# Second relational convolution of a graph network: running softmax maximum, attention dots from PSUM, first probabilities among the last product tiles

## The reference, cut to what matters

```python
def rgat_conv(x, W, q, k, b, src, dst, etype, heads, out_ch, n_nodes):
    xr = jnp.einsum('nd,rdf->rnf', x, W)
    oi = xr[etype, dst]
    oj = xr[etype, src]
    qi = oi @ q
    kj = oj @ k
    alpha = jax.nn.leaky_relu(qi + kj, NEG_SLOPE)
    m = jax.ops.segment_max(alpha, dst, num_segments=n_nodes)
    e = jnp.exp(alpha - m[dst])
    z = jax.ops.segment_sum(e, dst, num_segments=n_nodes)
    a = e / (z[dst] + EPS)
    msg = (a[:, :, None] * oj.reshape(-1, heads, out_ch)).reshape(-1, heads * out_ch)
    out = jax.ops.segment_sum(msg, dst, num_segments=n_nodes)
    return out + b
```

## Time and profile before

| | us |
|---|---|
| median of 3 runs | 1986.36 (1985.3 to 1987.12) |
| the profiled execution's own time | 1985.76 |
| its span | 1983.9 |
| PE busy | 1797.8 (91%) |
| DVE busy | 1300.2 (66%) |
| ACT busy | 725.5 (37%) |
| POOL busy | 711.7 (36%) |

### The profile page before, as it was taken

The page is one execution under the profiler, slowest core; times in us unless marked ns, Lnnn a source line. Parts: engine busy times, 40 slices in busy tenths (PEclk is TensorE's granted clock), DMA queues, the critical chain, the costliest instruction groups (busy, mean ns, idle before and its releaser), DMA issues. The chain is left out here.

```text
span 1983.9 us, 26904 instructions
## 1 busy us (share of the span) xinstructions
PE 1797.8 (91%) x8995; PEld 1504.9 (76%) x8997; DVE 1300.2 (66%) x2159; ACT 725.5 (37%) x1170; POOL 711.7 (36%) x386
## 2 busy tenths in 40 slices
PE   8999888999999998979886778688999999999887
PEld 3444685999999997868864578587788888899866
DVE  9998476887887886577399868665442422444545
ACT  0213544445444443323566534313224223332231
POOL 1665231422423331314766557311324233332411
PEclk9999999999999999979997889699999999999989
DMA  1002522222312221224200022012222222222230
GB/s 19 22 0 110 217 96 80 93 69 64 111 64 67 92 79 32 58 79 143 81 16 1 0 75 93 25 51 78 83 69 72 90 86 83 90 83 91 80 112 33
DMA packets 54199, 143.08 MB, mean 72 GB/s; under 512 B 13780, under 2 KB 13908, under 8 KB 53076
## 3 DMA queue, kind: packets, MB, share of 16 engines
q1 hardware_dynamic: 46898, 107.15, 17.5%
q10 hardware_dynamic: 7202, 34.63, 4.8%
HBM read 129.18 MB, written 12.58 MB: 71 GB/s over the span
## 5 line engine op out<-in xcount | busy, mean ns | idle before, releaser
L734 POOL TENSOR_TENSOR w_pair<-early,w_pair 128x768 fp32r<-128x768 f32 x234 | 450.2, 1953 | 921.0 <-ACT w_pair L1253 920.8
L789 PE MATMUL ps<-w_pair,cols_x 128*128 128x384 f32 x2160 | 390.8, 339 | 13.7 <-POOL cols_x L734 13.7
L789 PEld LDWEIGHTS ps<-w_pair,cols_x 128*128 128x128 f32 x2160 | 379.0, 190 | 18.5 <-POOL cols_x L734 14.1
L789 PE MATMUL ps<-w_pair,wide 128*128 128x384 f32 x1872 | 335.3, 339 | 13.1 <-DVE wide L1622 11.7
L789 PEld LDWEIGHTS ps<-w_pair,wide 128*128 128x128 f32 x1872 | 330.9, 191 | 17.5 <-DVE wide L1622 13.0
L1253 ACT ACTIVATE w_pair<-early 128x768 fp32r<-128x768 f32 x234 | 181.2, 840 | 341.8 <-PE ps L789 156.3
L1199 PE MATMUL ps<-wide,w_pair 128*128 128x512 f32 x972 | 224.9, 390 | 2.2 <-DVE wide L1622 2.2
L1199 PEld LDWEIGHTS ps<-wide,w_pair 128*128 128x128 f32 x972 | 181.5, 188 | 39.8 <-DVE wide L1622 2.6
L428 PE MATMUL count_ps<-early,src_hot 128*128 (+1 forms) x814 | 179.3, 382 | 7.9 <-DVE early L348 7.7
L428 PEld LDWEIGHTS count_ps<-early,src_hot 128*128 (+1 forms) x816 | 80.2, 98 | 106.5 <-issue 9.6
L1167 PE MATMUL ps<-prob,wide 128*128 128x512 f32 x588 | 149.4, 394 | 0.0
(11 more groups left out here) (239 smaller groups left out, 2450.6 us busy)
## 6 DMA issues: line engine op xcount, KB each, us to landing
early<-weights SPq DMA_DIRECT2D x240, 384.0 KB, 3.1
multi<-attn ACTq DMA_DIRECT2D x9, 768.0 KB, 4.5
...
kept<-early ACTq DMA_DIRECT2D x3, 1536.0 KB, 6.0
multi<-kept ACTq DMA_DIRECT2D x3, 1536.0 KB, 6.5
...
src_hot<-weights SPq DMA_DIRECT2D x10, 384.0 KB, 7.0
...
```

The lines of the kernel that those rows point to most:

```text
L734: return nc.gpsimd.tensor_tensor(dst, whole, high.bitcast(F32), ALU.subtract)
L789: mm = nc.tensor.matmul(ps[:, m, 0:HW], left[:, a, k, m * P:(m + 1) * P], w_pair[:, slot_of[0], b, k, :], start=(k == 0 and a + b == 0), s ...
```

## The change

Five things change in this layer:

1. **Dots from PSUM** (`product_dots` for `split_tile`): DVE reads bank m itself, after ACT's copies; the scratch output moves to `acc`. ACT no longer waits for the dots before it copies the next tile, and PE waits for the dots (`rows_ready`) before it writes a bank anew.
2. **Running maximum**: logits of relations 0 and 1 are finished among the tiles of relation 2, with the maximum of these two alone. The maximum with relation 2 (`greatest(2)`) comes during the row sums of relation 0. The difference of the two is exponentiated on ACT (`fade`), and scales the sums and denominators of relations 0 and 1 when those of relation 2 are added.
3. **Early u, v and probabilities**: u and v of relations 0 and 1 are transposed and spread among tiles 4 to 7 of relation 2; three exponents and two weighings of relation 0 stand among the dots of its tiles 6 and 7.
4. **Relation 2's source, maxima, u and v** move between the quarters of the row sums (`small` in `row_sums`), and DVE reads the banks in halves around its other work.
5. **Weights**: POOL's low parts of blocks 44 and 45, and ACT's high part of block 45, move behind the probabilities of relation 1. SP's load of a piece of block 45 follows POOL's piece of block 44, as before.

```diff
@@ uv_sets2
-        uv_sets2 = [(r_den[:], v_bc[:]), tuple(mask[:, 2 * i:2 * i + 2, :].rearrange("p m n -> p (m n)").bitcast(F32) for i in range(2))]
+        uv_sets2 = [(r_den[:], v_bc[:]), (acc_flat[:, 2 * D:2 * D + N], acc_flat[:, 2 * D + N:2 * D + 2 * N])]
@@ gpsimd
-                        if m == 3:
+                        if m == 3 and first_pass + 2 * r + n < 44:
                             weights_low(n, 3 * (first_pass + 2 * r + n))
...
+                if t == 2 * NB - 1:
+                    weights_low(0, 3 * 44)
+                    weights_low(1, 3 * 45)
@@ tensor
+                    if r or n:
+                        pe.wait_ge(rows_ready, 64 + 8 * r + 4 * n - 4 + m + 1)
...
-            for part in range(2):
-                max_round(12, 33, part)
-
-            pe.wait_ge(uv_ready, 11)
-            for r in range(REL3):
-                if r:
-                    pe.wait_ge(vb_ready, 21 + r)
-                turn_small(uvc[:, r, 0], 4)
-                pe.wait_ge(q_ready, 34 + r)
+                    if r == 2 and u == 4:
+                        pe.wait_ge(uv_ready, 11)
+                        turn_small(uvc[:, 0, 0], 4)
+                    elif r == 2 and u == 5:
+                        pe.wait_ge(q_ready, 33)
+                        spread_uv()
+                    elif r == 2 and u == 6:
+                        pe.wait_ge(vb_ready, 22)
+                        turn_small(uvc[:, 1, 0], 4)
+                    elif r == 2 and u == 7:
+                        pe.wait_ge(q_ready, 34)
+                        spread_uv()
...
+            row_sums(rows[0], prob_sets[0], 140, tile_copied, 109, 8, {2: last_source, 3: spread_last_source})
+            pe.wait_ge(den_read, 2)
+            pe.wait_ge(rows_low, 40)
+            row_sums(rows[1], prob_sets[1], 144, row_read, 13, 16, {1: turn_last_uv, 2: spread_last_uv})
@@ scalar
-                    copy_tile(38 + 2 * r + n, m, n, 88 + 8 * r + u, rows[r], lows=24 + 8 * r + u, dots_done=64 + 8 * r + u - 1)
-                    if m == 3:
+                    copy_tile(38 + 2 * r + n, m, n, 88 + 8 * r + u, rows[r], first=True, lows=24 + 8 * r + u)
+                    if m == 3 and 2 * r + n < 5:
                         split_high(40 + 2 * r + n, n)
...
+                    if r == 2 and u == 4:
+                        copy_rows(74, 4)
+                    elif r == 2 and u == 5:
+                        copy_uv(75, uv_sets2[0])
+                    elif r == 2 and u == 6:
+                        copy_rows(76, 4)
+                        exponentials(0, 0, 1)
+
+            exponentials(0, 1, NB + 1)
+            act.wait_ge(rows_ready, 88)
+            copy_uv(77, uv_sets2[1])
+            act.wait_ge(prod_done, 4 * 44)
+            exponentials(1)
+            copy_rows(78, 2)
+            split_high(45, 1)
+            act.wait_ge(fade_in, 1)
+            nc.scalar.activation(mx1[:, 1, 0], mx1[:, 1, 0], ACT.Exp).then_inc(fade, 1)
+            copy_rows(81, 4)
+            copy_uv(82, uv_sets2[0])
+            act.wait_ge(row_done, 16)
+            exponentials(2)
@@ vector
-                add(acc[:, m, part], acc[:, m, part], ps[:, m, 0:HW]).then_inc(row_read, 1)
+                nc.vector.scalar_tensor_tensor(acc[:, m, part], acc[:, m, part], mx1[:, 1, 0, m:m + 1], ps[:, m, 0:HW],
+                                               ALU.mult, ALU.add).then_inc(row_read, 1)
...
+            def product_dots(r, u):
+
+                n, m = u // 4, u % 4
+                part = slice(n * HW, (n + 1) * HW)
+                dve.wait_ge(tile_copied, 88 + 8 * r + u + 1)
+                dve.wait_ge(rows_ready, 64 + 8 * r + u)
+                for v in range(2):
+                    total = al1[:, v, r, 0, m:m + 1]
+                    start = 0.0 if n == 0 else al_part[:, v, m:m + 1]
+                    ins = dot(dot_scratch[v], ps[:, m, 0:HW], acc[:, v, part], start, al_part[:, v, m:m + 1] if n == 0 else total)
+                    ins.then_inc(rows_ready, 1) if v else mark(ins)
+                wait_steps()
...
+                    if r == 2 and u == 6:
+                        probabilities(0, 0, 2)
+                    elif r == 2 and u == 7:
+                        probabilities(0, 2, 3)
+                    product_dots(r, u)
                     if r and u == 2:
                         dve.wait_ge(rows_ready, 64 + 8 * r + u + 1)
-                        maxima(70 + 2 * (r - 1) + 1, mx1[:, r - 1, 0], 21 + r, 140)
+                        relation_logits(r - 1, 70 + 2 * (r - 1) + 1, 21 + r, 140)
+                        if r == 2:
+                            greatest(1)
+                            mark(relation_parts(0, mx[:]))
+                            relation_parts(1, mx[:]).then_inc(uv_ready, 1)
...
+            source_columns(al1[:, 0, 2, 0])
+            probabilities(0, 3)
+            probabilities(1)
+            read_denominators(79, True)
+            read_rows(0, range(NB))
             dve.wait_ge(mask_in, 16 * 6)
+            relation_logits(2, 80, 24, 148)
+            read_rows(0, range(NB, 8))
+            greatest(2)
+            sub(mx1[:, 1, 0], mx1[:, 1, 0], mx[:]).then_inc(fade_in, 1)
+            relation_parts(2, mx[:]).then_inc(uv_ready, 1)
+            read_denominators(83, False)
+            dve.wait_ge(row_read, 16)
+            read_rows(1, range(NB))
+            probabilities(2)
+            read_rows(1, range(NB, 8))
             dve.wait_ge(row_read, 24)
             add_bias_to_residual(1)
+            dve.wait_ge(fade, 1)
+            dve.wait_ge(den_read, 3)
+            mark(nc.vector.tensor_tensor(zc[:, 0], zc[:, 0], mx1[:, 1, 0], ALU.mult))
```

105 lines of the change are left out of this document (56 added, 49 removed).

## The result

| | before | after |
|---|---|---|
| median, us (4 runs each) | 1986.66 (1985.3 to 1987.12) | 1973.19 (1971.19 to 1973.69) |
| profiled execution, us | 1985.76 | 1973.41 |
| its span, us | 1983.9 | 1971.6 |

The ratio is 0.9934, with a 95% interval of 0.992 to 0.9948: faster by 0.7% (13.5 us), where 1.1% (20.6 us) was forecast. The measured time lies above the range of 1960 to 1972. The profiled execution is 8.4 us above the forecast of 1965.

What follows compares the result with a forecast made beforehand. PE bounds the products; behind them a chain through DVE, ACT and POOL does, up to the first row sums. Steps -4.3 - 22.5 + 1.0 + 2.5 + 2.3 + 0.4 = -20.6 take 1985.76 to 1965 us; range 1960 to 1972.

Steps and rivals of the forecast that it cites:

- Step A: Products of the second relational convolution: dots from PSUM bring kc earlier, inserts cost some back; last tile ends 4.3 us earlier.
- rival 3: Dots out of PSUM are held up by POOL too, giving 1974 us; chance 0.05.
- 0.5 us of each wait stay: PE's two waits for kc among the products, 2.8 us each before, shrink to 0.5 us each.
- Step B: Last tile to second half of first relation's row sums: 45.2 us become 22.7, half clock hidden in the wait; -22.5 us.
- Step C: Second half of the first relation's row sums: 1.0 us added for the clock, between 0 and 4.
- Step D: Second relation's row sums: 21.3 us become 23.8, with PE waiting for DVE's bank reads; +2.5 us, between 1.1 and 4.
- Step E: Third relation's start to normalization: DVE reaches the denominators 13.0 us after the start, behind the residual's load; +2.3 us.
- Step F: Eight fused multiply-adds from PSUM in place of adds, in a chain that DVE bounds; +0.4 us.
- Everything behind is unchanged: The part behind the normalization keeps its time; over 1 us of movement there would make the forecast wrong.
- The weights: Blocks 44 and 45 split behind POOL's probabilities cost nothing, with a cover of 6.5 us.
- rival 4: Slower: ACT, held by block 45, delays the third relation and everything behind, giving 1990 us; chance 0.03.
- Rival 1: DVE's short operations wait for POOL's (step B +2.8), half clock through step C's second half (3 more): 1971 us; chance 0.13.

Runs made afterwards that it cites:

- blocks_later: Changed kernel with the low parts of weight blocks 41 and 43 moved on GpSimd behind the next relation's first tile: 1964.52 us.
- kc_first: Changed kernel with kc (the source columns) made ahead of ks (the sources' scaling) on DVE: 1964.64 us.
- after_filled: Changed kernel with unread matmuls in six of PE's waits and no other edit: 1961.81 us.
- mends_and_fill: Changed kernel with blocks 41 and 43 later, banks read between the third relation's probabilities, residual loaded in halves, unread matmuls in six PE waits: 1958.63 us.
- fill_waits: Changed kernel with unread matmuls in two PE waits, 8 ahead of the third relation's sums and 30 ahead of the degrees: 1968.95 us.
- fill_tail: Changed kernel with unread matmuls, 50 and 9, in PE's two waits near the end: 1967.8 us.
- blocks_back: Changed kernel with weight blocks 44 and 45 split where they were before the change, among the last tiles: 1977.87 us.
- the filled kernels: Changed kernel and kernel before, with unread matmuls in six and five of PE's waits respectively, no other edits: 1961.81 and 1982.02 us.

## Why the prediction was wrong

By its own steps, against the profiled execution of the changed kernel:

- **Step A failed in size**: -1.6 us relative to the first product, forecast -4.3. The dots did what was said, 0.55 and 0.61 us whatever GpSimd did, so rival 3 is out. The wait for uv was 1.07 (1.0), and each tile with an insert took 3.4 us. What failed first is "0.5 us of each wait stay": they kept 1.22, which is 1.4 of the 2.7 us. The forecast took the small operations as they stand in the earlier trace rows, where the last of them took 0.91 us because GpSimd's block had just ended and it met a piece of a tile, half as long. Coming earlier, it met the last piece of the block and took 1.73. The forecast also said that these operations take up to 0.9 us each, but the cast in the earlier trace rows takes 1.77 alone. The sentence had the right place and read the rows as fixed durations. They were waiting times, and a chain that arrives earlier waits longer. The block was in view (blocks_later), and so was the move of ks (kc_first). Of the rest, 0.3 us is the tile behind the first transpose, which didn't get shorter (3.37 again), 0.2 is the dip of the clock, which had cost 1.5 and not 1.7, and some 0.6 are the inserts, whose tiles take 3.4 instead of 3.2 us.
- **Step B came near by two errors that go against each other**, which is luck: -23.7 (-22.5 forecast). The chain was 3.7 us shorter than the 22.7 us, 18.97 in after_filled: the second relation's first exponent began 9.1 us behind the last tile (11.2 forecast), and ACT's last high part ended 8.9 us behind that (10.2). But PE needed 17.7 us for its first half, two quarters of it at or near half clock, not 12 to 14, and so the wait of 3 us at the spread isn't there. "The half clock is hidden in that" was the wrong way round: the half clock hid the chain.
- **Step C**: +0.1 (1.0 forecast); with no wait ahead there was no dip. In mends_and_fill, where PE waited 2.09 us, the same 48 matmuls took 10.18 us, the forecast's case; but in after_filled, behind a wait of 2.06, they took 8.59, as if there had been none.
- **Step D held**: +2.4 (2.5), with the wait of 1.98 us at the denominators that was named.
- **Step E failed**: +4.8 (2.3). The residual's chain is right, 13.3 to 13.6 us in fill_waits, kc_first and after_filled. But PE, behind the 1.98 us of step D, ran two quarters at half clock and ended later than that chain. The forecast priced the wait of step D and not the clock behind it.
- **Step F**: +0.5 (0.4).
- **"Everything behind is unchanged" failed**: +1.6 us in the edge sums and +2.7 near the end, all of it half clock behind waits that are as long as before (the one ahead of the degrees is 0.5 us longer, 7.85 for 7.35). fill_tail took 4.15 us out there.
- **The weights**: GpSimd, the loads and ScalarE (ACT) ended in time, so rival 4 stayed out. ACT's parts of block 45, the factor and the row copy:

```profile
1265.89 0.84 ACT L1283 ACTIVATE w_pair<-early 128x768 fp32r<-128x768 f32 x1 [1.97 <-DMA early<-weights]
1269.06 0.21 ACT L1537 ACTIVATE mx<-mx 128x4 f32<-128x4 f32 x1 [2.33 <-DVE mx L1664]
1273.96 0.59 ACT L1283 ACTIVATE alpha<-ps 4x512 fp32r<-4x512 f32 x1 [4.69 <-PE ps L803]
```

ACT was free at 1269.3 and idle for 4.69 us: the cover held with less to spare than 6.5. What was missed is that the move shortens the chain at the maxima and frees GpSimd for the first probabilities (blocks_back).

With the start of the products, 0.9 us later in this execution, the deviations add up: 0.9 + 2.7 (A) - 1.2 (B) - 0.9 (C) + 2.5 (D to F) + 1.6 + 2.7 = 8.3, the 8.4 by which the profiled execution missed. Rival 1 had the right kind of cause and nearly the right time, 1971, but named the wrong places (locks in B, clock in C); the prediction gave it 0.13. The Trainium skill (TensorE: Matmul & The Clock Gate, Part 1) has the array at half clock after it has been idle, and the slow quarters behind the waits of 3.15 and 1.98 us agree. It also says that the number of slow matmuls varies from run to run of one kernel; the two profiles of the changed kernel don't show that, with every milestone within 0.1 us. What varies here is the loss from kernel to kernel. With the overlong fill and the loss near the end taken out, the filled kernels are 19.0 us apart, where the forecast was 20.6: there A gains 2.8 less than forecast, B and C gain 1.9 more, and E and F lose 0.6 more. So the steps' sum was 1.6 us off without most of the clock, by errors that partly cancel, and some 6 of the 8 us missing are the clock's (19.0 less 13.2). By the medians it is 6.7, a figure whose interval is some 4 us to either side. What stays open is why the same wait of 2 us costs 1.6 us of half clock in one kernel (kc_first: 3.55 for 2.33 and 1.34 for 0.95) and 4.7 in another (the changed one), and what decides it near the end; no run here separates that.
